# Two buffers for the one-hots, a gelu block in slot 10.5, and two unread products on TensorE

## The reference

```python
x = x + 0.5 * ffn(layernorm(x))        # f1
x = x + mamba(layernorm(x))            # p
x = x + 0.5 * ffn(layernorm(x))        # f2

def ffn(x):          # 8 experts, all computed, one taken for each token
    idx = argmax(softmax(x @ Wg + bg))
    h = gelu(einsum('th,ehi->tei', x, W1) + b1)
    y = einsum('tei,eih->teh', h, W2) + b2
    return y[token, idx]

def mamba(x):        # 256 channels, 16 states
    x_path, z = split(rmsnorm(x) @ in_proj.T)
    x_path = silu(causal_conv4(x_path))
    dt, B, C = split(x_path @ x_proj.T)
    dt = softplus(dt @ dt_proj.T + b)
    h_t = exp(dt_t * A) * h_{t-1} + dt_t * x_t * B_t    # over time
    y_t = sum_n(h_t * C_t) + D * x_t
    return (y * silu(z)) @ out_proj.T + x
```

## Time and the profile before

| | |
|---|---|
| median of 3 runs | 1493.84 us (1493.03 to 1496.21) |
| the profiled execution | 1495.2 us, span 1493.4 us |
| mean granted clock of PE | 0.849 |
| busy in the span: PE, DVE, ACT, POOL | 1232.2, 1061.7, 874.2, 1067.6 us |
| DMA | 130.02 MB, 87 GB/s in the mean |

### The profile page before, as it was taken

One profiled execution on the slowest core, in us unless ns is written; L12 is line 12 of the kernel. 1 busy time (PEld: TensorE's weight loads), 2 busy tenths in 40 slices (PEclk: granted clock), 3 DMA queues, 4 the chain that ended last, 5 costly groups with the idle time before them and its releaser, 6 DMA issues.

```text
span 1493.4 us, 16302 instructions
## 1 busy us (share of the span) xinstructions
PE 1232.2 (83%) x5188; PEld 612.7 (41%) x5188; DVE 1061.7 (71%) x1713; ACT 874.2 (59%) x1171; POOL 1067.6 (71%) x900
## 2 busy tenths in 40 slices
PE   2777768889898989989898988899898978667677
PEld 1333314234443534445353444444353434333344
DVE  2022887887878787877878787878878776979910
ACT  0244656476666767575667667575756675474532
POOL 1026796978878788868788787878687886997600
PEclk9989876788888998888888889888888987978786
DMA  3005050413233231503232332305032322232000
GB/s 84 1 0 205 10 198 9 158 43 120 92 108 106 89 111 33 181 23 127 80 120 92 108 106 73 127 24 185 28 115 85 122 85 105 101 114 92 1 7 14
DMA packets 60405, 130.02 MB, mean 87 GB/s; under 512 B 7744, under 2 KB 26864, under 8 KB 52128
## 3 DMA queue, kind: packets, MB, share of 16 engines
q1 hardware_dynamic: 60320, 128.98, 25.1%
HBM read 106.94 MB, written 22.02 MB: 86 GB/s over the span
## 4 chain that ended last, share of the span: by engine, by line
PE 41%; ACT 24%; DVE 23%; issue 8%; POOL 3%; SPq 1%; ACTq 0%; DVEq 0%; DMA 0%; POOLq 0%
PE PH L462 12%; PE PY L477 9%; DVE dA L759 9%; PE G L451 9%; ACT hs L610 6%; ACT dA L632 5%; DVE hb L757 4%; ACT hs L597 4%; DVE hb L763 3%; PE PH L461 3%; ACT L614 3%; ACT L610 2%; PE Y L489 2%; PE G L511 2%; PE G L531 2%
## 5 line engine op out<-in xcount | busy, mean ns | idle before, releaser
L936 POOL TENSOR_TENSOR hb<-dtx_rep,bs 128x1024 f32<-128x1024 f32 x256 | 598.8, 2361 | 0.0
L759 DVE TENSOR_TENSOR_SCAN dA<-dA,hb 128x512 f32<-128x512 f32 x352 | 429.8, 1221 | 68.5 <-ACT dA L632 61.6
L632 ACT ACTIVATE dA<-dt_rep,A 128x512 f32<-128x512 f32 x512 | 342.2, 689 | 143.4 <-DVE hb L763 128.7
L597 ACT COPY hs<-PH 128x512 f32<-128x512 f32 x256 | 149.4, 584 | 388.2 <-PE PH L462 387.9
L462 PE MATMUL PH<-xnT,W 128*128 128x512 f32 x512 | 339.0, 749 | 0.0
L477 PEld LDWEIGHTS PY<-W,hs 128*128 128x128 f32 x2048 | 281.8, 208 | 101.2 <-issue 88.8
L477 PE MATMUL PY<-W,hs 128*128 128x128 f32 x2048 | 323.2, 304 | 0.0
L944 POOL TENSOR_TENSOR hb<-hb,cs 128x1024 f32<-128x1024 f32 x80 | 188.4, 2355 | 140.7 <-DVE hb L757 140.7
L763 DVE TENSOR_TENSOR hb<-dA,cs 128x512 f32<-128x512 f32 x352 | 243.5, 692 | 25.2 <-DVE dA L759 0.9
L757 DVE TENSOR_TENSOR_SCAN hb<-dA,hb 128x512 f32<-128x512 f32 x160 | 186.3, 1206 | 102.6 <-ACT dA L632 99.5
L489 PE MATMUL Y<-hb,Sel 128*32 128x512 f32 x1024 | 164.5, 716 | 19.8 <-POOL hb L944 10.4
(11 more groups left out here) (85 smaller groups left out, 1190.7 us busy)
## 6 DMA issues: line engine op xcount, KB each, us to landing
dtx_rep<-dtx_rows SPq DMA_DIRECT2D x32, 1024.0 KB, 6.5
dt_rep<-dt_rows SPq DMA_DIRECT2D x32, 1024.0 KB, 8.2
bs<-bc_rows SPq DMA_DIRECT2D x64, 256.0 KB, 3.7
cs<-bc_rows SPq DMA_DIRECT2D x64, 256.0 KB, 4.5
dtx_rows<-dtx SPq DMA_DIRECT2D x32, 256.0 KB, 2.5
dt_rows<-dt SPq DMA_DIRECT2D x32, 256.0 KB, 2.6
X<-in_x SPq DMA_DIRECT2D x16, 256.0 KB, 3.0
out<-X SPq DMA_DIRECT2D x16, 256.0 KB, 2.4
```

The lines of the kernel that those rows point to most:

```text
L597: nc.scalar.copy(hs[:, w, e, :], PH[:, :]).then_inc(ph_free, 1)
L632: nc.scalar.activation(dA[u % NA][:, :], dt_rep[:, h, g, :], ACT.Exp, scale=A[:, h, g, q:q + 1]).then_inc(decay, 1)
L759: nc.vector.tensor_tensor_scan(a, a, x_in_hb, 0.0, ALU.mult, ALU.add).then_inc(scan, 1)
L936: nc.gpsimd.tensor_tensor(hb[:, s % HR], dtx_rep[:, h, 2 * m:2 * m + 2, :], bs[:, q, None, :].broadcast_to([P, 2, CH]), ALU.mult).then_inc ...
```

## The change

The gelu block of f2 goes from ACT's slot 7.5 to 10.5. The second products of f2 move from slots 10 to 15 to slots 13 to 15 and, in the next round, 0 and 1, and the addition of f2 to X from 1.5 to 2.5. `ohT` has a second buffer for each ffn, taken in turn by chunk. First products and their copies, bc, dt1, dt0, z1, the taps and the D products move by up to a few slots; the D product of h = 1 now starts the sum of the second half. Twice in each round, at the end of slots 1 and 10, PE multiplies the identity with four experts of W1 (128x512, f32) into a bank of `G` that the next stage of that bank writes anew; nobody reads it.

```diff
-STAGES = [("ln_f1", 3, 0, 1, 0), ("gate_f1", 3, 1, 2, 1), ("z0", 1, 0, 2, 2), ("z1", 1, 1, 3, 2),
-          ("out", -1, 0, 4, 1), ("oh_f1", 3, 1, 5, 1), ("bc", 1, 0, 6, 0), ("dt1", 1, 1, 6, 1),
-          ("dt0", 1, 0, 7, 0), ("ln_f2", -1, 1, 9, 0), ("gate_f2", -1, 0, 10, 1), ("oh_f2", -1, 1, 12, 0),
+STAGES = [("ln_f1", 3, 0, 1, 0), ("gate_f1", 3, 1, 2, 1), ("z0", 1, 0, 2, 2), ("z1", 1, 1, 3, 1),
+          ("out", -1, 0, 4, 1), ("oh_f1", 3, 1, 5, 1), ("bc", 1, 0, 5, 0), ("dt1", 1, 1, 6, 0),
+          ("dt0", 1, 0, 6, 1), ("ln_f2", -1, 1, 9, 0), ("gate_f2", -1, 0, 10, 1), ("oh_f2", -1, 1, 12, 0),
           ("ln_p", 2, 0, 13, 0), ("x1", 2, 1, 14, 0), ("x0", 2, 0, 14, 1)]
...
-ACT_AT = {"ln_f1": 1.5, "silu": 4.0, "bc": 6.0, "dt1": 6.5, "dt0": 7.0, "soft": 7.0, "gelu_f2": 7.5,
-          "ln_f2": 9.5, "ln_p": 13.5, "taps": 14.5, "gelu_f1": 15.5}
-DVE_AT = {"gated1": 1.5, "y_f2": 1.5, "gate_f1": 3.0, "out": 4.5, "oh_f1": 6.0, "stats_f2": 5.0, "gated0": 9.5,
+ACT_AT = {"ln_f1": 1.5, "silu": 4.0, "bc": 5.5, "dt1": 6.5, "dt0": 6.5, "soft": 7.0, "gelu_f2": 10.5,
+          "ln_f2": 9.5, "ln_p": 13.5, "taps": 14.0, "gelu_f1": 15.5}
+DVE_AT = {"gated1": 1.5, "y_f2": 2.5, "gate_f1": 3.0, "out": 4.5, "oh_f1": 6.0, "stats_f2": 5.0, "gated0": 9.5,
           "y_f1": 10.0, "stats_p": 10.5, "gate_f2": 11.0, "stats_f1": 12.0, "oh_f2": 13.0, "tap01": 15.0, "tap2": 15.5}
...
-SP_AT = {"x_out": 3, "x_in": 4, "bc": 6, "b0": 8, "dt": 9, "b1": 10, "c0": 10, "b2": 12, "c1": 12, "b3": 14, "dtx1": 14,
+SP_AT = {"x_out": 4, "x_in": 4, "bc": 6, "b0": 8, "dt": 9, "b1": 10, "c0": 10, "b2": 12, "c1": 12, "b3": 14, "dtx1": 14,
...
-W1_AT = [[(8, 2, 7, 3, 3), (9, 2, 9, 0, 3), *[(s, 0, s, 0, 3) for s in (10, 11, 12, 13, 14, 15)]],
-         [(15, 1, 15, 0, -1), (15, 2, 15, 1, -1), (15, 3, 15, 3, -1), (1, 0, 0, 0, -2), (2, 0, 2, 0, -2),
-          (3, 0, 3, 0, -2), (5, 0, 4, 2, -2), (6, 0, 6, 0, -2)]]
-
-W2_AT = [[(s, 1, 2) for s in (4, 6, 8, 8, 8, 9, 9, 9)],
-         [(s, k, -2) for s, k in ((10, 1), (11, 1), (12, 1), (13, 1), (14, 1), (14, 1), (15, 1), (15, 2))]]
+HOLD_AT = {(1, 3): ("gate_f1", 1), (10, 3): ("oh_f2", 1)}
+
+W1_AT = [[(8, 2, 8, 0, 3), (9, 2, 9, 0, 3), (10, 0, 10, 0, 3), (10, 2, 10, 3, 3),
+          *[(s, 0, s, 0, 3) for s in (11, 12, 13)], (14, 1, 14, 0, 3)],
+         [(15, 0, 15, 0, -1), (15, 1, 15, 0, -1), (15, 3, 15, 3, -1), (0, 2, 0, 1, -2), (2, 0, 2, 0, -2),
+          (3, 0, 3, 0, -2), (4, 0, 4, 0, -2), (5, 0, 6, 0, -2)]]
+
+W2_AT = [[(s, 1, 2) for s in (5, 7, 7, 8, 8, 8, 9, 9)],
+         [(13, 1, -2), (14, 1, -2), (15, 1, -2), (15, 2, -2), (0, 1, -3), (0, 1, -3), (1, 1, -3), (1, 1, -3)]]
...
-D_AT = {8: 0, 12: 1}
+D_AT = {(8, 1): 0, (10, 3): 1}
...
-        ohT = sb("ohT", [3 * E, 2, CH], BF16)
+        ohT = sb("ohT", [3 * E, 2, 2, CH], BF16)
...
-                nc.tensor.matmul(PH[:, :], Lm[:, e, :], ohT[:, w, :], start=True, stop=False)
+                nc.tensor.matmul(PH[:, :], Lm[:, e, :], ohT[:, w, (it.i0 + off) % 2, :], start=True, stop=False)
...
-                if q == 0:
-                    it.wait(pe, gated, off, HF, h)
+                if k == 0:
+                    it.wait(pe, gated, off, HF, 0)
...
-                                            start=q == 0, stop=q == NQ - 1)
+                                            start=k == 0, stop=q == NQ - 1)
...
+            def skip_term(it, h):
+                if h == 1:
+                    it.wait(pe, gated, 0, HF, 1)
+                nc.tensor.matmul(Y[:, :], Dd[:, h, :], xs[:, it.i0 % 2, h].rearrange("p b l -> p (b l)"),
+                                 start=h == 1, stop=False)
+
+            def hold_clock(it, name, n):
+                if not it.has(G_AT[name][1]):
+                    return
+                it.wait_free(pe, g_free, name)
+                for _ in range(n):
+                    nc.tensor.matmul(G[G_AT[name][0]][:, :], Id[:, :], W1[:, 0:CH // P, :], start=True, stop=True)
...
                     for k in (1, 2, 3):
+                        if (s, k) in D_AT and it.has(0):
+                            skip_term(it, D_AT[s, k])
                         for unit in w1_units(s, k):
                             first_product(it, *unit)
                         for unit in w2_units(s, k):
                             second_product(it, *unit)
+                        if (s, k) in HOLD_AT:
+                            hold_clock(it, *HOLD_AT[s, k])
...
                 if t == ACT_AT["taps"] and it.has(2):
-                    it.wait(act, summed, 0, 8, 6)
+                    it.wait(act, summed, 0, 8, 5)
...
-                it.wait(dve, w2_done[w], LN_OFF[w] - 1, E, 1)
+                it.wait(dve, w2_done[w], LN_OFF[w] - 2, E, 1)
                 it.wait_full(dve, g_full, name)
-                nc.vector.tensor_copy(ohT[:, w, :], Gb[b][0:3 * E, 0:CH]).then_inc(g_free[b], 1)
+                nc.vector.tensor_copy(ohT[:, w, (it.i0 + LN_OFF[w]) % 2, :], Gb[b][0:3 * E, 0:CH]) \
+                    .then_inc(g_free[b], 1)
```

More of the change, by code:

```diff
@@ L474, in second_product @@
                     if e == 0:
-                        nc.tensor.matmul(PY[:, P * j:P * (j + 1)], ohT[:, w, P * j:P * (j + 1)], b_part[:, 1, :],
-                                         start=j == 0, stop=False)
+                        nc.tensor.matmul(PY[:, P * j:P * (j + 1)], ohT[:, w, (it.i0 + off) % 2, P * j:P * (j + 1)],
+                                         b_part[:, 1, :], start=j == 0, stop=False)
                     last = nc.tensor.matmul(PY[:, P * j:P * (j + 1)], hs[:, w, e, P * j:P * (j + 1)], W2[:, e, :],
```

## The result

The changed kernel takes 1450.0 us (median of four runs, 1448.0 to 1462.2), the kernel before 1493.4; the ratio is 0.972, 95% interval 0.967 to 0.978. The forecast was 1451, within 1408 to 1494. A second set of runs, beside other kernels, gave 1459.3 (1457.4 to 1460.0), ratio 0.977 (0.974 to 0.979). So the sign and the size hold. The changed kernel's four runs of the first set lie within 14.2 us, and the medians of its two sets are 9.3 apart; the runs of the kernel before lie within 4.2 us in the first set and within 11.9 (eleven runs) in the second. The profiled execution of the changed kernel took 1448.0 us.

What follows compares the result with a forecast made beforehand. Bound: DVE's chain plus four waits, 82.4 us a round. Full-clock 76.9 plus 2.4 for a clock fall gives 79.3, 3.1 less; 14 rounds save 43, so 1495.2 becomes 1452, and 1451 for the median; range 1408 to 1494.

Steps and rivals of the forecast that it cites:

- The round as DVE's chain plus waits: A round of 82.4 us is 68.6 of DVE's own work plus 13.8 of waits, which fall to 8.3.
- The replay: Unit costs played through one changed round: DVE waits 2.7, 1.2, 1.2 and 2.7 us before slots 8, 9, 10 and 1.
- The forecast of 76.9 at full clock: The changed round without any fall of PE's clock: 76.4 us plus 0.5 for small waits.
- The gelu block and the copies behind it: f2 gelus at slot 10.5: the 4.23 us wait before slot 9 goes, 2.4 returns before slots 9 and 10.
- Taps: Convolution taps moved to slot 14.0: DVE's 2.29 us wait before the first tap goes, just.
- Two buffers: Second one-hot buffer: gains nothing alone, but spares DVE's copy a wait on the second product of f2, moved to slot 13.
- The fall at z1: PE waits 2.2 us before z1; half clock for 10 us in 7 of 10 rounds, 3.4 each: 2.4 a round.
- The second fall: Half clock behind the gelu block at 10.5: x1 and x0 3.4 us late, taps wait 3.0, round 83.3.
- the slower rival: Half clock also behind the gelu block in every round: 13 us more, 1507; chance 0.18.
- The sign that was named for being right: Clock falls once, just after z1; round 79 us, wait before slot 9 near 1, none before the taps.
- The unread products: Extra PE matmuls in slots 1 and 10: cost 0 where PE waits, up to 2.0 us delay at half clock.
- The count of rounds and the ends: 14 rounds hold both the moved gelu block and DVE's slots; at 3.1 us each, 43 us less.

## Why the prediction was right, point by point

- **The round as DVE's chain plus waits** held. The replay gave waits of 2.7, 1.2, 1.2 and 2.7 before slots 8, 9, 10 and 1; measured are 2.64, 1.15, 1.27 and 2.60 to 3.07. Small waits were put at 0.5 and are about 0.9. They were misread before the change too: five that sum to 1.3, not three that sum to 0.9, so DVE's own work is 68.1 us a round and not 68.6, and the two errors nearly cancel. The forecast of 76.9 at full clock can be tested on one round: round 3 of the kernel with slot 1's product only has full clock throughout and takes 77.0.
- **The gelu block and the copies behind it.** That 4.23 would go and 2.4 come back is right; put back to 7.5 the block brings 4.24. But the test says that more depends on it: 41 us, of which the waits before slots 9 and 10 explain 1.8 us a round.
- **Taps.** The 2.29 goes, but "just", with a margin of 0.1 in the replay. A late fall of 3 us still shows no wait before the taps (rounds 4 and 10), one of 7 us shows 1.33 and those of 10 us 2.7 and 3.7.
- **Two buffers.** Nothing alone, needed for the rest: right, and 78 us if they are missing.
- **The fall at z1.** It was forecast in 7 of 10 rounds for 10 us at 3.4. It comes in nine rounds of ten, lasts 3 to 7 us, and DVE waits 0.4 to 0.8 before the out addition, 2.0 in the longest, 0.9 in the mean. This term (2.4 a round) was nearly three times too large. Its length was taken from the earlier trace rows, another place with other work; why the stretch is shorter here is open.
- **The second fall** was the slower rival, at 6.4 a round in all rounds with the first. Its mechanism is real, with the wait before the taps at 2.7 to 3.7 where 3.0 was said, but at this price only in 2 and 4 of ten rounds (0.8 a round in the mean of the first trace). The sign that was named for being right, one fall a round just after z1, did not come: eight of ten rounds have a second stretch at half clock. The steady round of 78.6 to 79.9 is therefore near the 79.3 forecast in part from other terms than I had named.
- **The unread products** were costed at nothing. This step failed: the pair costs 10 to 19 us, that of slot 10 alone about 10, probably by moving the fall behind the wait for POOL. "Any fall they avoid" was the wrong question; which work the fall lands on is the better one.
- **The count of rounds and the ends.** I took 14 rounds and no cost outside. The ten steady rounds gain 3.8 each where 3.1 was forecast, the other five 22 together (round 0 loses 0.6, rounds 1 and 13 gain 7 and 9), and 12.8 us are lost in the first 157 us and after round 14. The errors have opposite signs: 43 was forecast and 47.2 measured in the span. That is partly luck. The kernels without products and with the gelu block at 7.5 have the late start too (157.1 and 156.8; all traces of changed kernels lie between 152.7 and 164.3, the three of kernels with the old order between 147.5 and 150.0). So it seems to come from the moved first and second products or the other small moves; which of them was not tested.

The Trainium skill's sentence that the ramp penalty is under 1% of a span (TensorE: Matmul & The Clock Gate, Part 1) is said of the warm-up of matmuls. The prediction took it for what the clock is worth in all, and so read it does not agree with this kernel before or after: the mean granted clock is 0.849 and 0.882. Yet the time follows the clock only where DVE waits for PE, and the kernel before with unread products has a higher clock and is slower.

## What to carry to other kernels

Write down the waits of the engine whose chain sets the round, and replay a move of work against them; here that gave each of the four large waits to within 0.1 us, 0.4 for one. Ask of an idle engine not how to fill its wait but what stands behind it: work that is put in to keep TensorE's clock up can cost time (here 10 to 19 us for the pair), perhaps by pushing the fall onto the products that the chain waits for, and the mean clock does not show it. Fill and drain have their own order of waits, and a move that helps the steady rounds has to be priced there as well.

## What the runs showed of the hardware that I had not expected

The clock fell after single waits of 2.1 and 2.5 us and after three of 1.1 to 1.6 close together, but not each time. PE waits 2.5 us before z1 in all ten steady rounds of the changed kernel, and in round 7 the clock stays full there; with slot 1's product only, round 3 has waits of 2.5, 2.1, 1.1 and 1.6 us and no fall at all.

The length of a stretch at half clock did not follow from PE's work either. Rounds 4 and 6 of the changed kernel have the same waits and the same products without a gap behind them, and the clock came back after 3 us in one and 10 in the other. What decides it is open. For a kernel this means that the same instructions gave rounds of 77.4 and of 82.2 us in one execution.
